# Second attention of a two-layer transformer kernel: transposes regrouped, value products behind scores, projections side by side

## The reference

```
K = einsum('bpd,ihd->biph', x, W_K)      # 16 heads of 64, 8 sequences of 512
Q = einsum('bpd,ihd->biph', x, W_Q)
V = einsum('bpd,ihd->biph', x, W_V)
scores = einsum('biph,biqh->biqp', K, Q)
scores = where(tril, scores, -1e10)
attn = softmax(scores / sqrt(64), axis=-1)
z = einsum('biph,biqp->biqh', V, attn)
out = einsum('bqf,df->bqd', z_flat, W_O)
```

## Time and profile before

| | |
|---|---|
| median of three timed executions | 1570.02 us |
| the profiled execution, its own time | 1551.31 us |
| its span, first to last instruction | 1550.1 us |
| PE busy | 1474.4 us (95%) |
| DVE busy | 1080.8 us (70%) |
| ACT busy | 950.4 us (61%) |
| POOL busy | 751.3 us (48%) |
| granted TensorE clock, mean | 0.998 |

### The profile page before, as it was taken

One profiled execution on the slowest core, in us unless ns is written; L12 is line 12 of the kernel. 1 busy time (PEld: TensorE's weight loads), 2 busy tenths in 40 slices (PEclk: granted clock), 3 DMA queues, 4 the chain that ended last, 5 costly groups with the idle time before them and its releaser, 6 DMA issues.

```text
span 1550.1 us, 26789 instructions
## 1 busy us (share of the span) xinstructions
PE 1474.4 (95%) x8976; PEld 881.0 (57%) x8976; DVE 1080.8 (70%) x3458; ACT 950.4 (61%) x2490; POOL 751.3 (48%) x1274
## 2 busy tenths in 40 slices
PE   4999999999999999998999999999999999998999
PEld 2433433443338999984565655656565565655566
DVE  5999999998964777447667677676767766673433
ACT  4578877887784334436757667575757657673221
POOL 7433655655545555653636455363635534342322
PEclk9999999999999999999999999999999999999999
DMA  7266555445325667750000000000000000020422
GB/s 140 61 155 149 120 130 138 89 110 141 99 95 185 203 201 237 261 172 5 15 1 12 5 4 11 1 15 1 15 1 8 8 1 2 1 56 1 96 69 55
DMA packets 72317, 118.95 MB, mean 77 GB/s; under 512 B 19178, under 2 KB 35820, under 8 KB 72172
## 3 DMA queue, kind: packets, MB, share of 16 engines
q0 software_dynamic: 34336, 67.70, 17.2%
q1 hardware_dynamic: 37408, 48.75, 10.8%
q10 hardware_dynamic: 436, 0.79, 0.2%
HBM read 77.83 MB, written 39.45 MB: 76 GB/s over the span
## 4 chain that ended last, share of the span: by engine, by line
PE 62%; DVE 22%; ACT 9%; issue 3%; POOL 3%; DMA 1%; ACTq 0%; POOLq 0%; DVEq 0%
DVE mx L1743 8%; PE bank L1354 6%; ACT ar L1582 6%; PE pS L1321 5%; PE bank L1334 4%; PE pS L1135 4%; PE bank L1164 4%; PE bank L1363 4%; PE pS L1240 4%; PE bank L1254 4%; PE pS L1241 3%; PE bank L1291 3%; PE bank L1306 3%; PE bank L1402 3%; PE bank L1155 2%
## 5 line engine op out<-in xcount | busy, mean ns | idle before, releaser
L2374 POOL TENSOR_SCALAR ar<-ar,rd 128x512 f32<-128x512 f32 (+3 forms) x512 | 264.0, 535 | 307.7 <-DVE rd L2104 307.5
L1582 ACT ACTIVATE ar<-ar,nm 128x512 f32<-128x512 f32 (+3 forms) x512 | 284.9, 558 | 165.3 <-DVE nm L2095 165.1
L1743 DVE TENSOR_REDUCE mx<-pS 128x1 f32<-128x512 f32 x512 | 322.3, 682 | 30.6 <-PE pS L1135 30.6
L2095 DVE CUSTOM_DVE_ANT_0 ar<-pS,maskf 128x512 f32<-128x512 f32 (+3 forms) x512 | 228.3, 483 | 17.2 <-PE pS L1321 15.2
L1492 ACT ACTIVATE ar<-bank 128x512 f32<-128x512 f32 x342 | 196.4, 599 | 53.9 <-PE bank L1155 51.6
L1135 PE MATMUL pS<-all_r 64*128 64x512 f32 x512 | 213.7, 486 | 6.5 <-DVE mx L1743 4.4
L1334 PE MATMUL bank<-identr,all_r 128*128 128x128 f32 x1280 | 200.1, 286 | 11.7 <-ACT ar L1592 6.9
L1334 PEld LDWEIGHTS bank<-identr,all_r 128*128 128x128 f32 x1280 | 132.5, 141 | 111.7 <-issue 79.1
L1135 PEld LDWEIGHTS pS<-all_r 64*128 64x128 f32 x512 | 90.3, 192 | 150.7 <-DVE mx L1743 143.9
L1321 PE MATMUL pS<-ar 64*128 64x512 f32 (+3 forms) x1024 | 172.7, 456 | 0.0
L1354 PE MATMUL bank<-ar 128*64 128x512 f32 (+3 forms) x1024 | 153.6, 443 | 0.6 <-ACT ar L1592 0.6
(11 more groups left out here) (284 smaller groups left out, 2701.5 us busy)
## 6 DMA issues: line engine op xcount, KB each, us to landing
rows_in<-zrow SPq DMA_DIRECT2D x16, 1024.0 KB, 5.3
ar<-gd SPq DMA_DIRECT2D x16, 512.0 KB, 6.5
all_r<-dk POOLq DMA_DIRECT2D x56, 128.0 KB, 3.8
dk<-xT SPq DMA_DIRECT2D x21, 256.0 KB, 3.1
dq<-xT SPq DMA_DIRECT2D x16, 256.0 KB, 4.0
rows_out<-ar SPq DMA_DIRECT2D x32, 128.0 KB, 1.7
all_r<-dq POOLq DMA_DIRECT2D x28, 144.0 KB, 3.8
all_r<-dq POOLq DMA_DIRECT2D x28, 128.0 KB, 3.4
```

The source lines that it names most:

```text
L1582: S.activation(p, p, ACT.Exp, bias=nm1[:, c:c + 1], scale=-1.0, accum_out=den1[:, c:c + 1]).then_inc(*s_e1.inc(u, a))
L1743: V.tensor_reduce(mx[Gr % 2][:, col:col + 1], bS[n % 3], AX.X, ALU.max, negate=True).then_inc(*s_mx.inc(Gr, c))
L2095: V.tensor_tensor_reduce(pr_[pi][:, 0:w], pS[u % 2][:, 512 * a:512 * a + w], maskf[:, 512 - w:512], -0.125, 3e38, ALU.add, ALU.min, accum_ ...
L2374: G.tensor_scalar(p, p, rd1[:, c + a:c + a + 1], 1.0, ALU.mult, ALU.mult).then_inc(*s_p1.inc(u, a))
```

## The change

The units of a pair come in the order 3, 1, 2, 0. So the first round has scores of 512 and 256 columns, the second of 384 and 128. Blocks 2 and 0 (384 and 128 columns) now share a bank: block 2 is turned into columns 0 to 383, block 0 into 384 to 511 (`turned_at`), one straight behind the other, without a wait between them for a copy; both copies wait for both. Block 1's transposes still wait for the copy of block 3, in whose columns they are written. In the first round the order is now scores, the eight transposes of blocks 2 and 0, queries, keys, `v1` or `op1`; in the second: scores, values, eight transposes (block 3), what is due beside it, four transposes (block 1). The last step of `v1` moves by one round.

```diff
-UNITS = [(b, r, qb) for b in range(NB) for r in range(8) for qb in (3, 0, 2, 1)]
+UNITS = [(b, r, qb) for b in range(NB) for r in range(8) for qb in (3, 1, 2, 0)]
-    V1_AT = (6, 8, 10, 12, 13, 14, 15, 16)
+    V1_AT = (6, 8, 10, 12, 13, 14, 15, 17)
...
             add("soft", u)
             add("exp1", u, 0)
-            r = 8 * b + k // 2 + 1
-            if k % 2 == 0 and r < 8 * NB:
-                add("heads", r // 8, r % 8, 0)
-        if old:
-            add("turnp", p, 0)
-            add("turnp", p, 1)
-        if now:
-            add("exp1", u, 1)
-            add("soft", u + 1)
-            if k % 2 == 0 and r < 8 * NB:
-                add("heads", r // 8, r % 8, 1)
-            add("exp1", u + 1, 0)
-            add("exp1", u + 1, 1)
-            add("norm", u)
-            add("norm", u + 1)
-        if x % 2 and 0 <= z < NU // 4:
-            for kb in range(4):
-                add("values", z, kb)
+        r = 8 * b + k // 2 + 1
+        if k % 2 == 0:
+            if old:
+                for a in range(2):
+                    add("turnp", p, a)
+                    add("turnp", p + 1, a)
+            if now:
+                add("exp1", u, 1)
+                add("soft", u + 1)
+                for a in range(2):
+                    if r < 8 * NB:
+                        add("heads", r // 8, r % 8, a)
+                add("exp1", u + 1, 0)
+                add("exp1", u + 1, 1)
+                add("norm", u)
+                add("norm", u + 1)
+        else:
+            if now:
+                add("exp1", u, 1)
+                add("soft", u + 1)
+                add("exp1", u + 1, 0)
+                add("exp1", u + 1, 1)
+                add("norm", u)
+                add("norm", u + 1)
+            if 0 <= z < NU // 4:
+                for kb in range(4):
+                    add("values", z, kb)
+            if old:
+                add("turnp", p, 0)
+                add("turnp", p, 1)
...
         if now:
             beside_round(k, b)
-        if old:
+        if old and k % 2:
             add("turnp", p + 1, 0)
             add("turnp", p + 1, 1)
...
+    def turned_at(u):
+
+        return 384 if u % 4 == 3 else 0
...
-                PE.wait_ge(*(s_td if a else s_ta).at(u - 1, a))
+
+                PE.wait_ge(*(s_td if a else s_ta).at(u - 2 if u % 4 == 3 else u - 1, a))
...
-                at_ = 128 * (qb - t if a else t)
+                at_ = 128 * (qb - t if a else t) + turned_at(u)
...
-            ACTE.wait_ge(*s_t1.at(u, 0))
+            ACTE.wait_ge(*s_t1.at(u + 1 if u % 4 == 2 else u, 0))
...
-            DVE.wait_ge(*s_t1.at(u, 1))
+            DVE.wait_ge(*s_t1.at(u + 1 if u % 4 == 2 else u, 1))
```

More of the change, by code:

```diff
@@ L1588, in turnp @@
             qb, i, w = UNITS[u][2], (u // 4) % 2, 128 * (UNITS[u][2] + 1)
-            ACTE.wait_ge(*s_t1.at(u, 0))
+            ACTE.wait_ge(*s_t1.at(u + 1 if u % 4 == 2 else u, 0))
             o = pT[i][:, 128 * qb:128 * qb + 512 * (qb + 1)].rearrange("p (t n) -> p t n", n=512)
             S.copy(o[:, :, 0:128],
-                   tbank[0][:, 0:w].rearrange("p (t n) -> p t n", n=128)).then_inc(*s_ta.inc(u, 0))
+                   tbank[0][:, turned_at(u):turned_at(u) + w].rearrange("p (t n) -> p t n", n=128)).then_inc(*s_ta.inc(u, 0))
         def values(pair, kb):
@@ L2109, in turnp @@
             qb, i, w = UNITS[u][2], (u // 4) % 2, 128 * (UNITS[u][2] + 1)
-            DVE.wait_ge(*s_t1.at(u, 1))
+            DVE.wait_ge(*s_t1.at(u + 1 if u % 4 == 2 else u, 1))
             V.tensor_copy(pT4[i][:, 3 - qb:4, w:w + 128],
-                          tbank[1][:, 0:w].rearrange("p (t n) -> p t n", n=128)).then_inc(*s_td.inc(u, 1))
+                          tbank[1][:, turned_at(u):turned_at(u) + w].rearrange("p (t n) -> p t n", n=128)).then_inc(*s_td.inc(u, 1))
         def op1(b):
```

## The result

The kernel after takes **1639.08 us** (median of four runs, 1633.14 to 1641.66) against 1568.45 for the kernel before on the same chip (four runs, 1562.9 to 1573.45): a ratio of 1.045 (95% interval 1.0418 to 1.0482), slower by 70.6 us. The forecast was 1622, with a range of 1580 to 1652. The profiled execution after took 1633.14 us, with a span of 1631.8, which is 81.7 more than the one before. In it the second attention, from the first score matmul to the last value matmul, lasts 1485.2 - 705.8 = 779.4 us against 708.3 before (696.5 to 1404.8): +71, which is the whole difference of the medians. The other 10.6 us lie in parts whose code is the same, and seem to belong to the chip and not to the change: the profile before is an execution from another chip, on which the kernel before has a median of 1552.32 us.

What follows compares the result with a forecast made beforehand. PE was taken to set the pace in the second attention. New waits, less old waits and saved PE steps, gave +6.7 us a full batch and +52 in all on the 1570.02 us median: 1622 us, range 1580 to 1652.

Steps and rivals of the forecast that it cites:

- wait ahead of `op1`: First round at k = 2: `op1` waits for DVE's copy of the queries and starts 1.1 us late.
- old waits that go: PE's waits in the kernel before, at k = 4, 6 and 8, would vanish: 2.8 us a batch.
- PE's own steps: PE's steps without waits, with fewer changes of tiling mode: 0.1 us a pair, 0.8 a batch saved.
- New wait 1: First round: `v1` waits for DVE's copy of the queries out of `misc`, 0.71 us in each of five rounds.
- New wait 2: Second round: block 1's four transposes wait for ACT's and DVE's copies of block 3; next scores 0.81 us later, sometimes more.
- The criterion on POOL: Sign against the forecast: it is wrong if the releasers of PE's idle time are POOL's products.
- The rival in which POOL is late: The eight transposes of blocks 2 and 0 wait for POOL, 1 us in half the pairs: 1652 us, chance 0.13.
- Waits at their lower bounds: Rival: both new waits come at their smallest, as DVE and ACT catch up: 1576 us, chance 0.17.
- The faster case: Rival: mode switches and old waits go and no new wait replaces them: 1543 us, chance 0.08.

Runs made afterwards that it cites:

- e3_bank: The kernel after, with block 1's transposes in free columns of `pS[1]`, so they needn't wait for block 3's copies; 1585.16 us, 1.019 of the kernel before.
- e10_behind: The kernel before, with only block 3's eight transposes and their copies moved behind the values in the second round; 1598.51 us, 1.030 of the kernel before.
- e2_cover: The kernel after, with the second round ordered as before: block 3's transposes, values, block 1's transposes; 1588.45 us, 1.021 of the kernel before.
- e5_bank_first: e3_bank, with the queries ahead of the transposes in the first round, as before; 1557.36 us, 1.003 of the kernel before.
- e11_block1_first: e5_bank_first, with block 1's four transposes and their copies ahead of block 3's eight; 1562.73 us, 0.998 of the kernel before.
- e1_misc: The kernel after, with DVE's copy of the queries ahead of the two 256-column masked scores; 1615.04 us, 1.039 of the kernel before.
- e9_together: The kernel before, with only the queries moved behind the six transposes of the first round; 1582.61 us, 1.018 of the kernel before.
- e6_cover_first: e2_cover, with the queries ahead of the eight transposes in the first round; 1560.35 us, 1.003 of the kernel before.

## Why the prediction was right, and by how much each term was off

The forecast was +52 us and the measured difference 70.6. For six batches, in us:

| term | forecast | measured |
|---|---|---|
| wait ahead of `v1` | 30 x 0.71 = 21.3 | 11.9 (28 times) |
| wait ahead of `op1` | 6 x 1.1 = 6.6 | 5.4 |
| waits for block 3's copies | the rest of the sum, 33.9 | 36.2 |
| values behind the copy of the keys | 0 | 1.2 |
| old waits that go | 6 x -2.8 = -16.8 | -11.7 + 0.1 |
| PE's own steps | 6 x -0.8 = -4.8 | +12.3, most of it the clock |
| together | 6 x 6.7 = 40.2 | 55.4 |

The mechanism was right: PE's order and the queues of ACT and DVE, with a wait for a copy at each of the two places; the second attention came to 779.4 us for about 755. That 52 came as near to 70.6 as it did is in part luck: wait 1 was 10.6 us too long in the sum, which hides some of the 25.8 us by which the other terms were too low.

- **New wait 1** was right in place, releaser and number, and too long: 0.43 us for 0.71. In the k = 10 pair the copy starts 3.77 after the round's first scores (3.85 forecast), and `v1` starts at 4.51 (4.70 forecast). PE itself was slower than summed: it had ended the keys at 4.16, not 3.99.
- **New wait 2** was right in place and in its total, but not in which copy ends it, and the waits are fewer and longer: 31 in six batches, 1.17 us each on average, for some 50 of 0.8 in all eight. The k = 10 pair: eight transposes at 3.37 after the second round's scores (3.37 forecast), ACT's copy from 4.40 to 4.98 (4.01 to 4.57 forecast), and 0.15 us behind it the four transposes, at 5.13; DVE's copy at 4.46 (4.28), head 1's two transposes at 5.30 (5.03), the next scores at 5.56 (5.33). The forecast had DVE's copy as the last; measured, ACT's releases the run. The chain through ACT's late exponentials was too short at k = 4: 11.32 for 10.5, with 2.20 us of idle time ahead of the four transposes. The sum had left out five small steps that DVE does beside the attention from the third batch on (L2140 to L2148); they take 931.50 - 930.26 = 1.24 us ahead of the second round's masked scores. The second batch has none of them: there the masked scores follow DVE's reciprocal straight away, the wait is 0.95 us and the pair lasts 10.07, 1.25 less. k = 6 came as forecast (12.1 for 12.0), k = 2 nearly (18.49 for 18.35), k = 8 to 14 within 0.2. DVE in the k = 4 pair of the third batch, and then of the second:

```profile
930.17 0.17 DVE L2121 RECIPROCAL rd<-den 128x2 f32<-128x2 f32 x1 [0.99 <-ACT ar L1599]
930.26 0.41 DVE L2140 TENSOR_TENSOR rr<-rr 128x32 f32<-128x32 f32 x1
...
931.50 0.55 DVE L2112 CUSTOM_DVE_ANT_0 ar<-pS,maskf 128x384 f32<-128x384 f32 x1
```

```profile
834.58 0.17 DVE L2121 RECIPROCAL rd<-den 128x2 f32<-128x2 f32 x1 [1.00 <-ACT ar L1599]
834.67 0.54 DVE L2112 CUSTOM_DVE_ANT_0 ar<-pS,maskf 128x384 f32<-128x384 f32 x1
```

- **The criterion on POOL was wrong, the mechanism not.** I had written that POOL's products as releasers would prove me wrong. The view named them, for 36.2 us; e3_bank took the wait away with POOL unchanged, and e10_behind made it with ACT named. The rival in which POOL is late falls with the same runs for the kernel after, where none of the 31 waits is in a first round; in e2_cover POOL is late, at another place. What I should have asked for is the end of the product of the very unit that is turned.
- **The old waits** were put at 2.8 us a batch, but the trace before has only 11.7 us of idle time on PE in six batches, 1.9 a batch, so 5.2 us of the saving weren't there to be had.
- **The saving on PE's steps** (0.1 us a pair) did not come. Without the half-clock stretches (six times 3.4 us at half, 10.2) PE is busy for 2.1 us more than before, not 4.8 less; in e5_bank_first, with the clock at 1.00, it is 0.8 less. So fewer changes between halves and the whole of the array save 0.02 us a pair there. In e11_block1_first it is 0.14 a pair.
- **The clock** was missing from the sum: about 8 us in the six batches, 11 in the attention. Without it the six batches are 47 us longer, where 40 were forecast.
- **The rivals.** Waits at their lower bounds would have given 1576, and the copies do end later than that. The faster case needed both copies to be early, and both are late.

One thing stays open. Whether the half-clock stretches follow from PE's idle time in the k = 2 pair is only argued: they come in the kernels in which that pair waits longest (after 2.3 us, e1_misc 1.6, e10_behind 1.4), and hardly where it waits 0.7 to 0.9 (none in e2_cover and e9_together, one in e3_bank). But the k = 4 pair fits nearly as well (2.2, 2.2 and 1.7 us in these three, 0.2 to 1.1 in the others, but 1.5 in e11_block1_first, which has no stretch), and of the six stretches in after only one begins straight behind a k = 2 pair. They come in only some of the batches with the same waits, and no run changed the clock alone.

## What to carry to other kernels

Joining runs of transposes saved PE 0.02 to 0.14 us a pair here and took away the work behind which their copies end (0.56 and 0.69 us for 0.34 us of transposes), so keep work between two runs into the same bank, or give the second another bank. A step that is moved on PE moves in every engine's list: work out for each what then stands ahead of the copy that PE wants next. Test a releaser's name by giving the waiting instruction other memory: if the named engine is the cause, the wait stays. And look at many waits of one kind: the true releaser ended at the same distance before the end of every one (here 0.14 to 0.15 us).

## What was not expected of the hardware

- In these traces the granted clock falls to about half for 3.4 us (or 6.8, 10.2) at a time. In after PE was busy for 81 to 88% of the pair ahead of each of the six. The same kernel had six and seven such stretches in the same six batches, in part at other places. Each costs about 1.4 us, where half of 3.4 would be 1.7: some of it is taken out of a wait (behind the stretch at 1221 us PE waits 2.02 us ahead of the four transposes, in the same pair of other batches 2.19).
- Outside the attention, in code that is the same in all kernels, both profiles of after have a stretch of 10.2 us at 460 us and e11_block1_first one of 17.1 us at 458; no other profile has one there. These three come from the chips on which the kernel before takes 1567 to 1568 us. With the later start of its attention, this is why the span of e11_block1_first (1563.9) is longer than before's while its attention is not (707.5 for 708.3 us); how much is the clock and how much the chip is open. Four profiles (e1_misc, e6_cover_first, e9_together, e11_block1_first) have a stretch of 37.6 us at 21 us, and in the first three the attention begins no more than 1.4 us later than before. So spans are compared by stretch.
